# A decoder layer on one core: the static list of steps is made by playing their phases on the engines

## The chip, the cores and the metric

The kernel runs on one core of a Trainium2 chip. The metric is the device time of one execution in microseconds (us), the median over runs. The engines are named as in the profile: PE is TensorE, DVE is VectorE, ACT is ScalarE, POOL is GpSimd, SP is SyncE (here only a queue of DMA starts).

## What is computed

x is (4, 256, 256), a context is (4, 256, 128), all float32. Three blocks follow each other, each with a residual and a layer norm:

```python
x = layernorm(x + delta_rule_attention(x))          # 16 heads of 16, per batch, recurrent over 256 positions
x = layernorm(x + ssm(context, gate=x))             # selective scan, 16 states, 256 channels, y * silu(x)
x = layernorm(x + moe(x))                           # 2 shared + 16 routed experts, top 4, hidden 176
```

The SSM takes the attention's result only as its gate, so its recurrence depends on the context alone and can run beside attention. The experts need both.

## The kernel before, in words

**Attention** is a chain of steps per batch b = 0..3 (`ATTENTION`, L63 to L70): k, v, b, ssk, q, ssq project and normalise; P0 to P3 make products inside chunks of 16 positions; move_a sends them through DRAM (SP, L503 and L506) so that solve0 to solve2 (DVE, L1319 and L1320, 60 pairs of small instructions for four batches) can invert a triangular matrix per chunk; move_t sends the result back; tile_t spreads it for PE; UW0, UW1, H, GQ0, GQ1 are packed 32x32 products (L630); S1 to S14 are the recurrence over chunks, each a PE product and an ACT copy; O0, O1 give the output; ms normalises it (DVE L1386), wo projects it, ln and lnorm are the layer norm. Batches 0 and 2 are one chain, 1 and 3 another; each chain has one set of buffers.

**The SSM** is 32 iterations (2 halves of tokens by 16 states). `pre i` makes the inputs of iteration i+1: PE broadcasts B (L616), ACT copies it (L952) and takes the decays' exponentials (L961), POOL multiplies (L549), two buffers deep. `scan i` is the recurrence on DVE (L1273) and PE's broadcast of C (L623), which waits for the product of the iteration before; `add i` is DVE's product with C (L1281) and the sum (L1287). `y_out` closes a half. In front stand stack, dt0, dt1 and begin.

**The middle** of half 0: gate (SiLU of x on ACT, a product on DVE), yT, ynorm, x3T, gates0 to gates7 (top 4 of 16 by comparing all pairs; DVE L1429 to L1467), split (x into high and low parts, ACT L1084 and DVE L1416). gates0 may not start before `("y_out", 1)` (`NEEDS`, L87), because it writes into the SSM's buffers. The middle of half 1 goes beside the experts (`SIDE`).

**Experts**: PE's `hidden` and `outputs` (L809 to L834), ACT L1113, DVE L1477 and L1481, POOL L570. Before them the weights w1 are split: ACT copies to w1_hi (L1051), POOL subtracts to w1_lo (L556). w1_hi lies on the SSM's buffers, so this waits for the last y_out. In the kernel before the ACT part stands inside step `("tile_s", 3)`, L1046 to L1051.

**The order of the work.** Every engine's queue is written out in program order from one list, `STEPS = order()` (L122), and each engine takes from a step what is its own, so a DVE instruction that waits holds all later DVE instructions of the list. `order()` (L96) keeps one clock `now`. Each step has a PE time and a lateness; `now` goes on by the PE time and the chain may go on when `now` has passed its lateness:

```python
c = min(open_, key=lambda c: (max(ready[c], now), ["mid", "ssm", 0, 1].index(c)))
name, which, pe, late = chains[c].pop(0)
now = max(now, ready[c]) + pe
ready[c] = now + late
```

Ties go to the middle, then the SSM, then attention. SSM_PERIOD = 3.5 after each add, SECOND = 15 before chain 1 starts. `bank_turns()` (L127) follows the same list to give out PSUM banks.

Of the kernel before, what the change touches and what calls it, by code (L numbers as in the profile page):

```python
# [82 lines left out]

SSM_START = [("stack", 0, 3.5), ("dt0", 0.9, 8), ("dt1", 0.9, 12), ("begin", 0.5, 0.5)]
MIDDLE = [("gate", 0, 4), ("yT", 2, 3), ("ynorm", 0, 1), ("x3T", 2, 2)] + [(f"gates{i}", .2, 2) for i in range(GATE_PARTS)] + [("split", 0, 0)]

NEEDS = {"gate": {("lnorm", 0), ("lnorm", 1), ("y_out", 0)}, "gates0": {("y_out", NG - 1)}}  # L87

# [5 lines left out]


def order():  # L96

    chains = {x: [(n, b, pe, late) for b in range(x, B, 2) for n, pe, late in ATTENTION] for x in range(2)}  # L100
    chains[0] = chains[0][PRELUDE:]
    chains["ssm"] = [(n, 0, pe, late) for n, pe, late in SSM_START] + [s for i in range(NITER) for s in
                     [("pre", i, .5, 0), ("scan", i, .5, 0), ("add", i, 0, SSM_PERIOD)] + [("y_out", i // DS, 0, 4)] * (i % DS == DS - 1)]
    chains["mid"] = [(n, 0, pe, late) for n, pe, late in MIDDLE]
    ready = {0: 0, 1: SECOND, "ssm": 0, "mid": 0}
    done, steps, now = set(), [], 0
    while any(chains.values()):
        open_ = [c for c in chains if chains[c] and (c != "mid" or NEEDS.get(chains[c][0][0], set()) <= done)]
        c = min(open_, key=lambda c: (max(ready[c], now), ["mid", "ssm", 0, 1].index(c)))
        name, which, pe, late = chains[c].pop(0)  # L110
        now = max(now, ready[c]) + pe
        ready[c] = now + late
# [6 lines left out]

SECOND = 15  # L120
SSM_PERIOD = 3.5
STEPS = order()  # L122
MID_NAMES = [n for n, _, _ in MIDDLE]
SSM_NAMES = [n for n, _, _ in SSM_START] + ["pre", "scan", "add", "y_out"]


def bank_turns():  # L127
# [72 lines left out]
def decoder_layer(nc, x_tok_d, x_t_d, ctx_t_d, wqkvb_d, onorm_d, wo_d, inproj_d, convw_d, convb_d, xproj_d,  # L200
# [7 lines left out]
    with ExitStack() as ctx:  # L208
# [367 lines left out]
        def _(pe):  # L576
# [312 lines left out]
        def _(act):  # L889
# [23 lines left out]
            def prelude():  # L913
# [11 lines left out]
                for name, _, _ in ATTENTION[:PRELUDE]:  # L925
                    step(name, 0)
# [42 lines left out]
            def step(name, b):  # L969
# [74 lines left out]
                if name == "ln":  # L1044
                    rstd(x)
                if (name, b) == ("tile_s", B - 1):  # L1046

                    act.wait_ge(s_yout, 2 * NG)
                    act.wait_ge(s_ld_w1, LD_W1)
                    for kt in range(KT):  # L1050
                        act.activation(w1_hi[:, kt, :], w1[:, kt, :], ACT.Copy).then_inc(s_w1hi, 1)  # L1051

# [106 lines left out]
        def _(dve):  # L1159
# [47 lines left out]
            def prelude():  # L1207
# [24 lines left out]
                for name, _, _ in ATTENTION[:PRELUDE]:  # L1232
                    step(name, 0)
# [280 lines left out]
            for name, which in STEPS:  # L1514
# [10 lines left out]
                elif name == "y_out":  # L1525
                    y_out(which)
                elif name in MID_NAMES:
                    middle(name, which)
                elif name != "pre":
                    step(name, which)  # L1530
# [88 lines left out]
```

## Time and profile before

| what | us |
|---|---|
| median of 3 runs | 677.39 (673.43 to 677.89) |
| the profiled execution, its own time | 676.46 |
| its span in the trace | 674.7 |
| DVE busy | 427.9 (63%) |
| PE busy | 413.5 (61%) |
| ACT busy | 235.7 (35%) |
| POOL busy | 187.2 (28%) |
| chain that ended last: DVE, PE, issue, ACT | 50%, 25%, 10%, 8% |

Read it in stages. Up to 92 us inputs are loaded and the SSM is prepared beside the first attention steps; up to 345 us the 32 scans run with attention between them; up to 481 us attention of batches 2 and 3 runs with the middle; then the experts run to the end.

### The profile page before, as it was taken

The page shows a single profiled execution, that of the slowest core. Times are in us where ns is not written, and L with a number is a line of the kernel's source. Part 1 is how long each engine was busy: PE and PEld are TensorE (multiplying, and loading weights), DVE is VectorE, ACT ScalarE, POOL GpSimd, SP SyncE. Part 2 cuts the span into 40 slices and gives each one's busy share as a digit, 9 for nine tenths or more (in the row PEclk, how much of TensorE's full clock was granted, in tenths as well). Part 3 has the DMA queues.
Part 4 walks back from the last instruction along what each step waited for, and adds up shares of the span by engine and source line. Part 5 has one row for each costly group of instructions (what it writes and reads, how often), then busy time and mean ns, then how long its engine had stood idle before and what let it go on. Part 6 is the DMA issues. An engine that isn't in the chain of part 4 may idle for free.

```text
span 674.7 us, 18534 instructions
## 1 busy us (share of the span) xinstructions
PE 413.5 (61%) x8286; PEld 308.6 (46%) x8286; DVE 427.9 (63%) x608; ACT 235.7 (35%) x425; POOL 187.2 (28%) x100
## 2 busy tenths in 40 slices
PE   5656234612566646440578561654498999999994
PEld 3334122401343424220365450553376777778883
DVE  3554889999999987999865644210655566453334
ACT  3556245322334264531344521115243422122220
POOL 1000024421354433421200000005554563334441
PEclk9865757555555576655757555655689989999998
DMA  8001011001000000100100012502300000000000
GB/s 255 2 2 33 0 34 26 12 1 32 3 4 4 1 2 2 35 1 17 16 2 6 3 36 70 196 4 74 125 0 1 1 1 1 0 33 1 1 1 31
DMA packets 27962, 18.05 MB, mean 27 GB/s; under 512 B 19873, under 2 KB 25835, under 8 KB 27627
## 3 DMA queue, kind: packets, MB, share of 16 engines
q1 hardware_dynamic: 27723, 16.84, 8.4%
q8 instruction: 65, 1.06, 0.7%
q0 software_dynamic: 160, 0.04, 0.1%
q14 instruction: 14, 0.11, 0.1%
HBM read 13.66 MB, written 3.21 MB: 25 GB/s over the span
## 4 chain that ended last, share of the span: by engine, by line
DVE 50%; PE 25%; issue 10%; ACT 8%; POOL 2%; DMA 2%; SPq 1%; DVEq 1%; POOLq 0%; ACTq 0%
DVE arena_h L1273 12%; DVE arena_h L1287 8%; DVE arena_h L1281 6%; PE bank L630 4%; PE bank L834 3%; DVE tmp_o L1319 3%; DVE tt_s L1320 2%; PE bank L809 2%; PE bank L810 2%; PE bank L811 2%; POOL hg_lo L570 2%; PE bank L829 2%; PE bank L830 2%; DVE hg_hi L1481 2%; DVE ln_st L1191 1%
## 5 line engine op out<-in xcount | busy, mean ns | idle before, releaser
L549 POOL TENSOR_TENSOR arena_s<-du,bsb 128x1024 f32<-128x1024 f32 x32 | 86.3, 2696 | 240.9 <-ACT bsb L952 183.3
L570 POOL TENSOR_TENSOR hg_lo<-vkp,hg_hi 128x512 fp32r<-128x512 f32 x50 | 69.0, 1380 | 91.0 <-DVE hg_hi L1481 91.0
L1273 DVE TENSOR_TENSOR_SCAN arena_h<-arena_s 128x1024 f32<-128x1024 f32 x32 | 82.2, 2569 | 1.9 <-DVE ln_mv L1195 0.7
L1477 DVE TENSOR_TENSOR vkp<-vkp,bank 128x512 f32<-128x512 f32 x50 | 34.4, 687 | 72.0 <-ACT vkp L1113 71.3
L630 PE MATMUL bank<-vkp,tiles 32*32 32x32 f32 (+1 forms) x3072 | 52.6, 222 | 33.3 <-ACT tiles L966 20.6
L1113 ACT ACTIVATE vkp<-bank,b 128x512 f32<-128x512 f32 x50 | 34.3, 686 | 109.1 <-PE bank L811 108.8
L630 PEld LDWEIGHTS bank<-vkp,tiles 32*32 32x32 f32 x3072 | 47.3, 145 | 41.9 <-ACT tiles L966 22.8
L1287 DVE TENSOR_TENSOR arena_h<-arena_h 128x1024 f32<-128x1024 f32 x30 | 54.7, 1822 | 4.4
L623 PE MATMUL bank<-stk,eye 96*128 96x512 bf16 x32 | 18.8, 587 | 56.1 <-DVEq L1283 56.1
L961 ACT ACTIVATE arena_s<-delta,negA 128x510 f32<-128x510 f32 x64 | 42.3, 711 | 25.3 <-DVEq L1274 25.3
L556 POOL TENSOR_TENSOR w_lo<-w,w_hi 128x3200 fp32r<-128x3200 f32 x2 | 13.8, 6925 | 132.3 <-ACT w_hi L1051 132.3
L830 PE MATMUL bank<-w_lo,hg_hi 128*128 128x256 f32 x200 | 49.9, 283 | 0.0
L630 PE MATMUL bank<-qke,tiles 32*32 32x48 f32 (+1 forms) x1984 | 35.9, 233 | 20.6 <-issue 8.1
L630 PEld LDWEIGHTS bank<-qke,tiles 32*32 32x32 f32 x1984 | 32.7, 149 | 27.5 <-issue 17.7
L630 PE MATMUL bank<-tt_s,tiles 32*32 32x16 f32 x896 | 22.8, 212 | 35.5 <-ACT tt_s L1026 26.4
L1281 DVE TENSOR_TENSOR arena_h<-arena_h,bank 128x1024 f32<-128x1024 f32 x32 | 39.1, 1221 | 6.6 <-PE bank L623 2.1
L809 PE MATMUL bank<-x_hl,w_hi 128*128 128x512 f32 x100 | 41.9, 419 | 0.0
L810 PE MATMUL bank<-x_hl,w_hi 128*128 128x512 f32 x100 | 40.8, 408 | 0.0
L630 PEld LDWEIGHTS bank<-tt_s,tiles 32*32 32x32 f32 x896 | 17.2, 142 | 50.9 <-ACT tt_s L1026 32.7
L811 PE MATMUL bank<-x_hl,w_lo 128*128 128x512 f32 x100 | 40.4, 404 | 0.0
L830 PEld LDWEIGHTS bank<-w_lo,hg_hi 128*128 128x128 f32 x200 | 38.0, 190 | 1.0
L654 PE MATMUL bank<-xT,wqkvb 128*128 128x256 f32 x96 | 30.5, 479 | 9.1 <-DVEq L1175 9.1
(195 smaller groups left out, 851.8 us busy)
## 6 DMA issues: line engine op xcount, KB each, us to landing
w<-in_w SPq DMA_DIRECT2D x1, 3200.0 KB, 12.0
w<-in_w SPq DMA_DIRECT2D x3, 512.0 KB, 9.1
xT<-in_x_t SPq DMA_DIRECT2D x1, 1024.0 KB, 7.2
xres<-in_x_tok SPq DMA_DIRECT2D x1, 1024.0 KB, 8.8
scr_a<-at_g SPq DMA_DIRECT2D x4, 256.0 KB, 2.0
at_g<-scr_a SPq DMA_DIRECT2D x32, 32.0 KB, 2.1
scr_t<-tt_s SPq DMA_DIRECT2D x4, 256.0 KB, 2.0
at_g<-scr_t SPq DMA_DIRECT2D x32, 32.0 KB, 2.0
```

The lines of the kernel that those rows point to most:

```text
L549: pool.tensor_tensor(dBu[:, i % 2, :].rearrange("p (e t) -> p e t", e=2), du[:, :, GT_ * th:GT_ * th + GT_], bsb[:, i % 2, :].unsqueeze(1) ...
L570: pool.tensor_tensor(hg_lo[i % 2][:, :], hrel[:, i % 2, :], hg_hi[i % 2][:, :], ALU.subtract).then_inc(s_hglo, 1)
L630: mm = pe.matmul(o[r, at], tiles[x][k][r, half, c, :, :].rearrange("p g n -> p (g n)"), moving[r], start=start, stop=stop, skip_group_chec ...
L809: pe.matmul(o[:, :], w_hi, x_hl[th][:, 0, kt, :], start=(kt == 0), stop=False)
L810: pe.matmul(o[:, :], w_hi, x_hl[th][:, 1, kt, :], start=False, stop=False)
L811: mm = pe.matmul(o[:, :], w_lo, x_hl[th][:, 0, kt, :], start=False, stop=(kt == KT - 1))
L830: pe.matmul(o, h_hi, w_lo, start=False, stop=False, skip_group_check=True)
L961: act.activation(o, src, ACT.Exp, scale=negA[:, et, n:n + 1]).then_inc(s_dA, 1)
L1273: link(dve.tensor_tensor_scan(hst, dA[:, i % 2, :], dBu[:, i % 2, :], 0.0, ALU.mult, ALU.add))
L1281: link(dve.tensor_tensor(h_c, hst.rearrange("p (e t) -> p e t", e=2), bank_c[:, :].unsqueeze(1).broadcast_to([P, 2, GT_]), ALU.mult))
L1287: link(dve.tensor_tensor(ysum, ysum, hC, ALU.add))
L1477: link(dve.tensor_tensor(h, h, o[:, :], ALU.mult))
```

## The change

The two numbers beside each step are gone. A table `PHASES` gives for each step a sequence of stays on engines, and `order()` plays them: it keeps one clock for each of PE, ACT and DVE, and for each chain when its last step was issued and complete. It always takes the step that can start earliest; ties go to chain 0, chain 1, the SSM, the middle, w1. The split of w1 becomes a step of its own, after the last y_out. In every engine's code only the names follow; the instructions of a step are the same.

```diff
-SSM_START = [("stack", 0, 3.5), ("dt0", 0.9, 8), ("dt1", 0.9, 12), ("begin", 0.5, 0.5)]
+SSM_START = ["stack", "dt0", "dt1", "begin"]
+PHASES = {"k": "pe 2.6 act .8", "v": "pe 2.6 act 2.1 dve .9", "b": "pe 2.6 act 3.3", "ssk": "pe 1.5 dve .8 act 1.6 dve 1.7",
...
+          "tile_u": "act 1.5", "P": "pe 1.5 dve .7 act 1.1", "move_a": "dma 9.5", "move_t": "dma 9.5",
+          "solve0": "dve 4.9", "solve1": "dve 4.3", "solve2": "dve 6.8",
+          "UW": "pe 2 dve .8 act .5", "H": "pe 2.6 act .3", "GQ": "pe 2 dve 1.4", "S": "pe .5 act .3", "base": "pe 3", "O0": "pe 1.6",
...
+          "pre": "pe .6 act 2.1", "scan": "dve 2.5", "add": "dve 3.1", "y_out": "dve 1.6",
...
+EARLY = {"q", "P1", "P2", "P3", "UW1", "GQ0", "GQ1", "tile_u", "tile_s", "O1", "wo"} - {"wo"}
...
+NEEDS = {"gate": {("lnorm", 0), ("lnorm", 1), ("y_out", 0)}, "gates0": {("y_out", NG - 1)},
+         "w1": {("ln", B - 2), ("y_out", NG - 1)}}
...
+    chains["w"] = [("w1", 0)]
+    rank = [0, 1, "ssm", "mid", "w"]
+    engine = dict.fromkeys(["pe", "act", "dve", "dma"], 0.0)
...
+    def start(c):
+        name, which = chains[c][0]
+        at = issued[c] if name in EARLY else complete[c]
...
+        work = phases(name)
+        return max(at, engine[work[0][0]]) if work and work[0][0] != "dma" else at
+
     while any(chains.values()):
-        open_ = [c for c in chains if chains[c] and (c != "mid" or NEEDS.get(chains[c][0][0], set()) <= done)]
-        c = min(open_, key=lambda c: (max(ready[c], now), ["mid", "ssm", 0, 1].index(c)))
+        open_ = [c for c in rank if chains[c] and NEEDS.get(chains[c][0][0], set()) <= done]
+        c = min(open_, key=lambda c: (start(c), rank.index(c)))
...
+        for e, us in phases(name):
+            at = (max(at, engine[e]) if e != "dma" else at) + us
+            if e != "dma":
+                engine[e] = at
...
-                if (name, b) == ("tile_s", B - 1):
-
-                    act.wait_ge(s_yout, 2 * NG)
...
+            def split_w1():
+                act.wait_ge(s_yout, 2 * NG)
...
+                elif name == "w1":
+                    split_w1()
```

What the list becomes (both lists follow from the code by themselves):

| where in the list | before | after |
|---|---|---|
| scan 0 stands behind | solve2 of batch 0 | solve2 of batch 0 and P3 of batch 1 |
| last step of batch 0 (lnorm) stands behind | add 19 | add 5 |
| last step of batch 1 | add 30 | scan 11 |
| last step of batch 2 | the middle, no scan left | scan 17 |
| last step of batch 3 | the end of the list | add 25 |
| move_a, move_t of batch 3 | no scan left | add 15, scan 17 |
| scans with no attention between them | none | 27 to 31 |
| ynorm, x3T, gates0 to gates7, split | beside attention of batches 2 and 3 | the end of the list, alone |
| ACT's split of w1 | behind tile_s of batch 3 | right behind y_out 1 |

In the new list some attention steps stand next to each other on DVE with no scan between them: solve0 to solve2 of batch 0 around P of batch 1; solve0, solve1, UW, solve2, GQ (batches 1 and 0) with no scan before scan 1; solve0 to solve2 of batch 2 and of batch 3; UW, ssk, GQ of batches 2 and 3 before scan 13.

## Rows read from the trace of the kernel before

**Rows 1.** Windows: length, busy us of PE, PEld, DVE, ACT, POOL, then clock, DMA, GB/s.
```profile
0.00:92.40 92.40, 47.16 (x355) 27.09 (x355) 49.81 (x91) 43.35 (x66) 6.07 (x12) 0.76 0.19 57
92.40:345.00 252.60, 118.18 (x3757) 79.52 (x3757) 230.82 (x237) 100.23 (x200) 83.56 (x31) 0.57 0.05 11
345.00:486.00 141.00, 80.52 (x3186) 65.10 (x3186) 52.87 (x110) 42.70 (x89) 14.69 (x3) 0.56 0.19 62
481.40:674.70 193.30, 172.27 (x1004) 140.05 (x1002) 96.78 (x179) 51.42 (x75) 83.71 (x56) 0.96 0.02 6
```

**Rows 2.** Waits of DVE from 345 to 486 us: total, times, longest.
```profile
DVE tmp_o L1386 <- ACT v_w L1043: 34.9, 2, 24.8
DVE tiles L1374 <- PE bank L630: 14.3, 2, 11.6
DVE tmp_o L1319 <- DMA at_g<-scr_a: 9.1, 1, 9.1
```

**Rows 3.** The same of DVE from 92.4 to 345 us, its longest.
```profile
DVE arena_h L1281 <- PE bank L623: 2.1, 1, 2.1
```

**Rows 4.** Timeline of DVE: an iteration, ms of batch 0, a scan, ms of batch 3.
```profile
165.73 2.29 DVE L1273 TENSOR_TENSOR_SCAN arena_h<-arena_s 128x1024 f32<-128x1024 f32 x1
...
169.54 2.13 DVE L1287 TENSOR_TENSOR arena_h<-arena_h 128x1024 f32<-128x1024 f32 x1
171.70 2.29 DVE L1273 TENSOR_TENSOR_SCAN arena_h<-arena_s 128x1024 f32<-128x1024 f32 x1
...
221.20 0.75 DVE L1386 SCALAR_TENSOR_TENSOR tmp_o<-tmp_o,onorm,v_w 128x512 f32<-128x512 f32 x1
221.87 4.44 DVE L1273 TENSOR_TENSOR_SCAN arena_h<-arena_s 128x1024 f32<-128x1024 f32 x1
...
471.47 6.68 DVE L1386 SCALAR_TENSOR_TENSOR tmp_o<-tmp_o,onorm,v_w 128x512 f32<-128x512 f32 x1 [24.84 <-ACT v_w L1043]
```

**Rows 5.** Timeline of POOL: beside that scan, the w1 subtractions, the first of w2.
```profile
221.56 2.60 POOL L549 TENSOR_TENSOR arena_s<-du,bsb 128x1024 f32<-128x1024 f32 x1 [1.48 <-ACT bsb L952]
...
463.78 13.82 POOL L556 TENSOR_TENSOR w_lo<-w,w_hi 128x3200 fp32r<-128x3200 f32 x2 [132.31 <-ACT w_hi L1051]
485.12 4.16 POOL L563 TENSOR_TENSOR w_lo<-w,w_hi_b 128x512 fp32r<-128x512 f32 x2 [7.53 <-ACT w_hi_b L1102]
```

**Rows 6.** Timeline of PE: H of batches 0 and 3, scores, first hidden, first outputs.
```profile
120.29 3.38 PE L630 MATMUL bank<-k_uv,tiles 32*32 32x16 f32 x237 [2.40 <-ACT k_uv L1013]
125.29 0.50 PE L630 MATMUL bank<-k_uv,tiles 32*32 32x16 f32 x19 [1.62 <-issue]
...
349.33 3.59 PE L788 MATMUL bank<-cent,xT 128*128 128x16 f32 x16
...
429.84 0.73 PE L630 MATMUL bank<-k_uv,tiles 32*32 32x16 f32 x39 [1.36 <-ACT k_uv L1013]
...
436.20 1.37 PE L630 MATMUL bank<-k_uv,tiles 32*32 32x16 f32 x89 [1.55 <-issue]
...
481.43 0.99 PE L809 MATMUL bank<-x_hl,w_hi 128*128 128x512 f32 x1
...
489.71 0.36 PE L829 MATMUL bank<-w_hi_b,hg_hi 128*128 128x256 f32 x1 [3.49 <-DVE hg_hi L1481]
```

**Rows 7.** Timeline of ACT: table load before the sigmoid, split of w1.
```profile
353.01 1.28 ACT L1092 ACT_TABLE_LOAD   x1 [2.37 <-PE bank L788]
...
460.76 5.61 ACT L1051 ACTIVATE w_hi<-w 128x3200 fp32r<-128x3200 f32 x2
```

**Rows 8.** Timeline of DVE: a comparison of gates0, the first copy of gates6, split.
```profile
354.82 1.22 DVE L1430 TENSOR_TENSOR du<-sc 128x1024 f32<-128x1024 f32 x1
...
380.72 0.69 DVE L1458 CAST stk<-bank 96x512 bf16<-96x512 f32 x1 [1.70 <-ACT wb L1096]
...
387.62 1.22 DVE L1416 TENSOR_TENSOR x_hl<-xT,x_hl 128x1024 fp32r<-128x1024 f32 x1 [2.09 <-ACT x_hl L1084]
```

**Rows 9.** Costliest groups: the scans; busy, mean ns of one, idle before.
```profile
L1273 DVE TENSOR_TENSOR_SCAN arena_h<-arena_s 128x1024 f32<-128x1024 f32 x32 | 82.2, 2569 | 1.9 <-DVE ln_mv L1195 0.7
```

More of the change, by code:

```diff
@@ L82 @@
 GATE_PARTS = 8
-SSM_START = [("stack", 0, 3.5), ("dt0", 0.9, 8), ("dt1", 0.9, 12), ("begin", 0.5, 0.5)]
-MIDDLE = [("gate", 0, 4), ("yT", 2, 3), ("ynorm", 0, 1), ("x3T", 2, 2)] + [(f"gates{i}", .2, 2) for i in range(GATE_PARTS)] + [("split", 0, 0)]
-NEEDS = {"gate": {("lnorm", 0), ("lnorm", 1), ("y_out", 0)}, "gates0": {("y_out", NG - 1)}}
+SSM_START = ["stack", "dt0", "dt1", "begin"]
+MIDDLE = ["gate", "yT", "ynorm", "x3T"] + [f"gates{i}" for i in range(GATE_PARTS)] + ["split"]
+PHASES = {"k": "pe 2.6 act .8", "v": "pe 2.6 act 2.1 dve .9", "b": "pe 2.6 act 3.3", "ssk": "pe 1.5 dve .8 act 1.6 dve 1.7",
[6 rows of a table added]
+          "pre": "pe .6 act 2.1", "scan": "dve 2.5", "add": "dve 3.1", "y_out": "dve 1.6",
+          "gate": "act 3.9 dve 1.7", "yT": "pe 2 dve 3.8 act .6", "ynorm": "dve 2", "x3T": "pe 2 act 1.3",
+          "gates0": "pe 2 act 2.8 dve 1.5", "gates6": "pe .8 act .7 dve 2", "gates": "dve 1.4", "split": "act 1.1 dve 1.3"}
+EARLY = {"q", "P1", "P2", "P3", "UW1", "GQ0", "GQ1", "tile_u", "tile_s", "O1", "wo"} - {"wo"}
+INPUT_LAG = 1.9
+ROWS_OF_C = .6
+NEEDS = {"gate": {("lnorm", 0), ("lnorm", 1), ("y_out", 0)}, "gates0": {("y_out", NG - 1)},
+         "w1": {("ln", B - 2), ("y_out", NG - 1)}}
 SIDE = dict(zip([1, 3, 4, 6, 8, 10, 11, 12, 13, 14, 15, 17, 18],
@@ L93, with phases @@
 LAST_NORM_AT = 3
+def phases(name):
+    for key in (name, name.rstrip("0123456789")):
+        if key in PHASES:
+            words = PHASES[key].split()
+            return [(e, float(us)) for e, us in zip(words[::2], words[1::2])]
+    return []
 def order():
-    chains = {x: [(n, b, pe, late) for b in range(x, B, 2) for n, pe, late in ATTENTION] for x in range(2)}
+    chains = {x: [(n, b) for b in range(x, B, 2) for n in ATTENTION] for x in range(2)}
     chains[0] = chains[0][PRELUDE:]
-    chains["ssm"] = [(n, 0, pe, late) for n, pe, late in SSM_START] + [s for i in range(NITER) for s in
-                     [("pre", i, .5, 0), ("scan", i, .5, 0), ("add", i, 0, SSM_PERIOD)] + [("y_out", i // DS, 0, 4)] * (i % DS == DS - 1)]
@@ L104, in order @@
-    chains["mid"] = [(n, 0, pe, late) for n, pe, late in MIDDLE]
-    ready = {0: 0, 1: SECOND, "ssm": 0, "mid": 0}
-    done, steps, now = set(), [], 0
-    while any(chains.values()):
-        open_ = [c for c in chains if chains[c] and (c != "mid" or NEEDS.get(chains[c][0][0], set()) <= done)]
-        c = min(open_, key=lambda c: (max(ready[c], now), ["mid", "ssm", 0, 1].index(c)))
-        name, which, pe, late = chains[c].pop(0)
-        now = max(now, ready[c]) + pe
-        ready[c] = now + late
+    chains["ssm"] = [(n, 0) for n in SSM_START] + [s for i in range(NITER) for s in
+                     [("pre", i), ("scan", i), ("add", i)] + [("y_out", i // DS)] * (i % DS == DS - 1)]
@@ new lines, in order @@
+    chains["mid"] = [(n, 0) for n in MIDDLE]
+    chains["w"] = [("w1", 0)]
+    rank = [0, 1, "ssm", "mid", "w"]
+    engine = dict.fromkeys(["pe", "act", "dve", "dma"], 0.0)
+    issued, complete = dict.fromkeys(rank, 0.0), dict.fromkeys(rank, 0.0)
+    inputs, scanned = {0: 0.0}, 0.0
+    done, steps = set(), []
+    def start(c):
+        name, which = chains[c][0]
+        at = issued[c] if name in EARLY else complete[c]
+        if name == "pre":
+            at = max(issued[c], scanned)
+        if name == "scan":
+            at = inputs[which]
+        work = phases(name)
+        return max(at, engine[work[0][0]]) if work and work[0][0] != "dma" else at
@@ new lines, in order @@
+    while any(chains.values()):
+        open_ = [c for c in rank if chains[c] and NEEDS.get(chains[c][0][0], set()) <= done]
+        c = min(open_, key=lambda c: (start(c), rank.index(c)))
+        at = start(c)
+        name, which = chains[c].pop(0)
+        issued[c] = at
+        if name == "scan":
+            engine["pe"] = max(engine["pe"], complete[c]) + ROWS_OF_C
+        if name == "add":
+            at = max(at, engine["pe"])
+        for e, us in phases(name):
+            at = (max(at, engine[e]) if e != "dma" else at) + us
+            if e != "dma":
+                engine[e] = at
+        if name in ("begin", "pre"):
+            inputs[which + (name == "pre")] = at + INPUT_LAG
+        if name == "scan":
+            scanned = at
+        if name != "pre":
+            complete[c] = max(complete[c], at)
@@ L118 @@
 PRELUDE = 6
-SECOND = 15
-SSM_PERIOD = 3.5
 STEPS = order()
-MID_NAMES = [n for n, _, _ in MIDDLE]
-SSM_NAMES = [n for n, _, _ in SSM_START] + ["pre", "scan", "add", "y_out"]
+MID_NAMES = MIDDLE
+SSM_NAMES = SSM_START + ["pre", "scan", "add", "y_out", "w1"]
 def bank_turns():
@@ L1528, in _ @@
                     middle(name, which)
-                elif name != "pre":
+                elif name not in ("pre", "w1"):
                     step(name, which)
```

21 lines of the change are left out of this document (10 added, 11 removed), and 7 rows, old and new, of tables (ATTENTION, PHASES).

## The prediction

> **What bounds the kernel now.** I read the page first, then the windows by stage, then who waits for whom, then the timelines. The busy shares say little: DVE has 63% and PE 61%, and neither is full. The windows split it [rows 1]. From 92.4 to 345 us DVE is busy 230.8 of 252.6 us, 91%: all 32 scans run there, and DVE is the bound. From 345 to 486 us it is busy 52.9 of 141 us, 37%, and PE 57%: here no engine is full, and the latency of attention's chain for batch 3 is the bound. The waits of the second stage say so: DVE waited 34.9 us for ACT's result of ms, 14.3 us for GQ on PE and 9.1 us for the DMAs of move_a [rows 2], while the longest wait of the first stage was 2.1 us [rows 3]. From 481.4 us on the experts run, PE busy 172 of 193 us. So the order before spends its scans early, and when the last two batches wait for PE, ACT and DMA, nothing is left to fill DVE. That is where an order can gain: bring attention's latencies under the scans. It can't gain in the experts, and not below DVE's work.
>
> **The change, part by part.** No instruction is added or taken away. What changes is what stands behind what, on all queues. I work out when y_out 1 ends (call it T), then what stands between T and the experts, then the total.
>
> *Up to scan 0.* DVE reaches scan 0 at 92.4 us now, with 49.8 us of work [rows 1]. The new list puts P0 to P3 of batch 1 ahead of it; these are eight DVE instructions of some 0.29 us, 2.3 us. PE makes them while DVE solves batch 0, so I add only the 2.3: 94.7 us. Everything else of this stretch is the same work, and the ACT latencies of dt0 and dt1 stay open in it.
>
> *DVE's work from there to T.* Before, DVE did 230.8 + 52.9 = 283.7 us between 92.4 and 486 [rows 1]. From this come off: 2.3 for P of batch 1; 5.9, since ms of batch 3 took 6.68 us where ms of batch 0 takes 0.75 (it stood against POOL's w1 subtraction, which ran from 463.78 to 477.6) [rows 4, 5]; and 15.2 for what now stands behind T: ynorm 1.3, gates0 to gates4 6.4 (five of 1.22 and one of 0.23), gates5 2.0, gates6 1.7, gates7 1.8, split 1.2, and 0.8 of gaps counted with them (the pieces are the DVE rows from 354.56 to 388.84 that belong to gates and split, the dearest and the last stand in [rows 8]). Left: 260.3 us. In the dense stage DVE did its work at 91.4% [rows 1], the rest being the ends of instructions and short waits. At the same density 260.3 us take 285 us.
>
> *The waits that are new.* Batches 0 to 2 are now denser, so DVE meets waits that scans covered before. I follow the new list with these durations: H about 5.5 us from its release (120.29 to 125.8) [rows 6], GQ half of H, ms 9 to 10 us from the start of O0 (210.5 to 221.2 for batch 0) [rows 4], a move 7 to 10 us (DVE waited 9.1 for one) [rows 2], an iteration 5.97 us (165.73 to 171.70) [rows 4]. GQ of batch 0 stands right behind solve2 of batch 1 and comes 3.7 us late; GQ of batch 1 4.4; ms of batch 0 5.8 (only add 4 covers it), its wo 1.4; P of batch 2 2.0; ms of batch 1 1.0; GQ of batch 2 5.3 (only ssk of batch 3 covers H); P of batch 3 2.7; ms of batch 2, gate and yT together 5.0; UW of batch 3 and smaller ones 3.3; GQ of batch 3 3.5. That is 38 us. H took 7.8 us for batch 3 where PE showed pauses called issue (429.84 to 437.57) [rows 6], against 5.5 for batch 0; I add 5 us for such pauses in four batches. The extremes: at 0 the scans cover it all, and T is 380; at the density of the second stage now (37%) for all the attention work, there would be over 100 us of waits. I take 43, nearer to the first, since 26 of 32 adds still stand between attention steps, and no single wait before was longer than 2.1 us where scans stood between [rows 3].
>
> T = 94.7 + 285 + 43 = 422.7 us.
>
> *The tail of the list.* Between T and the experts nothing is left for overlap, while now gates run beside attention. ACT starts the split of w1 at T and POOL's subtractions start 3.0 us later and end at T + 16.8 (460.76, 463.78, 477.6) [rows 5, 7]. They don't bound: PE's first expert product needs also split, and that is a chain: ynorm 1.3; x3T behind ACT's 5.6 us of w1, to T + 7; scores 3.6 on PE [rows 6]; table load and sigmoid 1.5 [rows 7], so gates0 could start at T + 12.5. Its comparison has two operands in SBUF. The scan beside which POOL's product started 0.3 us earlier took 4.44 instead of 2.29 us [rows 4, 5], and ms took 6.68 instead of 0.75, until the subtraction was over. So I let gates0 wait for POOL: end of its first comparison T + 18.1, gates1 to gates4 T + 23.1, gates5 T + 25.3, gates6 with PE's transposes and ACT's copy 4.1 (T + 29.4), gates7 T + 31.3, split T + 33.6 (ACT's copy and DVE's 1.22, 2.3 from 386.53 on) [rows 8]. PE starts at T + 34 = 456.7 us, where it starts at 481.4 now [rows 6]: 24.7 us earlier. Without POOL's hindrance it would be T + 29.5, 4.5 us less.
>
> The Trainium skill, SBUF — State Buffer, Who interferes with whom, says that DVE and GpSimd share a port pair which one instruction holds for its whole length, the other being blocked fully. By that rule gates0 waits for the second subtraction to end, which is what I took from the two rows; by a rule of shared bandwidth the comparison would take about double, 1.2 us more, and the forecast would be 3 us lower. The trace agrees with the lock: 6.68 us ended 0.5 us after POOL did.
>
> *Behind it.* ACT's first split of w2 now starts before PE's first product, since nothing of attention stands in front, and the 4.16 us of POOL [rows 5] are out of the way sooner: outputs(0) comes 5 us behind the first product instead of 8.3 (481.4 to 489.7) [rows 6]: 3.3 us. The loads of w1 and w2 start earlier and were hidden. The experts are 193.3 us of the same instructions at clock 0.96.
>
> **Sum.** 676.46 - 24.7 - 3.3 = 648.5 us for an execution like the profiled one. That one is 0.93 us under the median, so 649.4; I say **649 us**, 4.2% less.
>
> **The rivals.**
>
> *A, the scans cover nearly everything.* The waits are under 20 us instead of 43, as in the dense stage now. For it: the longest wait there was 2.1 us [rows 3]. Against: there one or two attention steps stood between scans, now in places over ten. T = 380 to 395, the total 607 to 625.
>
> *B, slower: DVE stands in its own order.* DVE is in order. Wherever the table's time for PE is short of the chip's, a GQ or ms stands at the head of DVE with scans ready behind it, and no wait overlaps another. The table has 2.6 us for H, the trace 5.5 to 7.8 [rows 6]; UW, GQ, O and wo are short in the same way. In place of the 43 us put x: the kernel is slower when T passes 450.7, at x = 71, which is 18 us per batch. For it: the second stage shows 60 us of waits for two batches [rows 2], which nothing covered; all four batches at half of that give 120 x 0.6 = 72. Against: 26 iterations lie between. At x = 90 the total is 696. It decides with the tail: of the 105 us that batch 3 had alone, 34 come back behind T.
>
> *C, the scans get longer.* The 32 scans average 2.57 us where an undisturbed one takes 2.29 [rows 4, 9], 9 us in all; the one of 4.44 had POOL's product started just before it. The rule just cited speaks for more of these: the pre steps now stand behind attention's ACT work, so products start late. If every second scan pays 2.15 us, it is 34 us instead of 9: 25 more, total 674, no change to be told. Against: with nothing between, the iteration settles with POOL beside the adds, at 5.97 us [rows 4].
>
> *D, the change doesn't do what it says.* The chains don't run ahead on the chip as they do in the table, since the PE times in it are too short, and batch 3 ends late, with fewer scans beside it and S steps that wait for PE's broadcast of C. Half of the gain: 660 to 668.
>
> **How the numbers follow.** The forecast with its waits of 25 to 60 us (631 to 666): 0.55. A: 0.13. B: 0.13. C: 0.09. D: 0.10. A measurement of this kernel can tell about 1% from no change, 6.8 us. Faster by over 1% (under 670.6): all of the forecast, A, D and a third of C, 0.81. Within 1%: the rest of C and the near edge of B, 0.07. Slower by over 1%: 0.12. Leaving out the lower half of A and most of B gives 617 to 678.
>
> **What would show it.** In the new profile: scan 0 at about 95 us; the last scans 5.6 to 6.0 us apart with nothing of attention between them; L1386, L1374 and L1319 with several DVE waits of 1 to 6 us instead of few of 9 to 25; y_out 1 at 423 us, L1051 right behind it; one comparison of gates0 lengthened by POOL; PE's first L809 34 us later; experts of 190 us. I am wrong if DVE's share from scan 0 to y_out is over 87% (A) or under 74% (B), if the mean of L1273 goes over 3 us (C), or if y_out 1 comes before 450 us and the total is still not lower: then the tail or the experts have taken it.

## The result, and the profile after

The changed kernel is slower: 700.59 us, median of 4 runs (700.39 to 703.15), against 676.74 us for the kernel before, timed beside it. The ratio is 1.037, interval 1.0325 to 1.0414. The forecast was 649 us, its range 617 to 678. The profiled execution took 700.67 us with a span of 698.9, and what follows is compared with the 676.46 us and the span of 674.7 shown before.

The windows of the profile after, by stage (each row: length; busy time and number of instructions of PE, PE's weight loads, DVE, ACT, POOL; PE's granted clock; DMA share; GB/s). They are cut at scan 0, at the end of y_out 1 and at PE's first expert product:

```profile
0.00:102.20 102.20, 51.41 (x612) 31.25 (x612) 55.54 (x98) 51.78 (x84) 8.00 (x12) 0.75 0.19 54
102.20:476.60 374.40, 184.22 (x6644) 134.08 (x6644) 267.79 (x309) 125.36 (x262) 76.35 (x30) 0.56 0.10 30
476.60:510.50 33.90, 6.58 (x29) 5.74 (x29) 18.82 (x30) 12.51 (x11) 14.59 (x3) 0.50 0.00 0
510.50:698.90 188.40, 171.14 (x1002) 139.49 (x1002) 92.07 (x172) 49.67 (x72) 83.47 (x56) 0.96 0.02 6
```

In [rows 1] there was one stage with DVE at 91% and one with DVE at 37%. Now both are gone. Scans and attention lie over each other for 374 us, and DVE is busy 267.8 us of them, 71.5%. That is far from the 91% at which DVE was the bound: 106.6 us of DVE stand empty. The balance to the kernel before: scan 0 9.8 us later (102.2 for 92.4), from scan 0 to the experts 408.3 us for 389.0, so 19.3 more, and the experts 4.9 us shorter (188.4 for 193.3). 9.8 + 19.3 - 4.9 = 24.2, the difference of the spans.

The waits of DVE from 102.2 to 476.6 us, where before they were those of [rows 2] and [rows 3] (total, times, longest):

```profile
DVE tiles L1420 <- PE bank L675: 39.2, 8, 10.7
DVE tmp_o L1432 <- ACT v_w L1088: 18.9, 4, 7.6
DVE vkp L1404 <- PE bank L675: 5.7, 4, 2.0
DVE tiles L1414 <- PE bank L675: 5.0, 2, 2.6
```

L1420 is GQ's step on DVE (L1374 before), L1432 that of ms (L1386 before). The long wait of ms for batch 3, 24.8 us, and the 9.1 us for move_a are gone, as the change intends. In their place every batch waits for GQ, twice: 39.2 us in 8 waits, where the two batches of [rows 2] had 14.3. The timeline of DVE shows how these holes look: GQ of batch 1 and ms of batch 0, with the product with C and the sum of one iteration between them and no scan; then the longest wait, GQ of batch 2, and the scan behind it:

```profile
164.58 0.88 DVE L1420 SCALAR_TENSOR_TENSOR tiles<-bank,const 128x256 f32<-128x256 f32 x2 [8.09 <-PE bank L675]
...
169.09 0.88 DVE L1420 SCALAR_TENSOR_TENSOR tiles<-bank,const 128x256 f32<-128x256 f32 x2 [3.31 <-PE bank L675]
...
180.62 0.75 DVE L1432 SCALAR_TENSOR_TENSOR tmp_o<-tmp_o,onorm,v_w 128x512 f32<-128x512 f32 x1 [7.59 <-ACT v_w L1088]
181.29 2.28 DVE L1319 TENSOR_TENSOR_SCAN arena_h<-arena_s 128x1024 f32<-128x1024 f32 x1
...
289.72 0.88 DVE L1420 SCALAR_TENSOR_TENSOR tiles<-bank,const 128x256 f32<-128x256 f32 x2 [10.71 <-PE bank L675]
...
294.98 2.29 DVE L1319 TENSOR_TENSOR_SCAN arena_h<-arena_s 128x1024 f32<-128x1024 f32 x1 [0.22 <-DVE qke L1423]
```

The scans at 181.29 (scan 5) and 294.98 (scan 13) are the point. The first starts as ms ends, with no wait of its own. The last part of a scan's input is POOL's product, and POOL's timeline has those of scan 5 and scan 13:

```profile
154.53 4.09 POOL L594 TENSOR_TENSOR arena_s<-du,bsb 128x1024 f32<-128x1024 f32 x1 [10.18 <-ACT bsb L997]
...
262.95 2.35 POOL L594 TENSOR_TENSOR arena_s<-du,bsb 128x1024 f32<-128x1024 f32 x1 [19.93 <-DVEq L1320]
```

So the input of scan 5 was there from 158.6 us and that of scan 13 from 265.3. Both scans were ready for the whole of the 7.59 us and of the 10.71 us, and stood in DVE's queue behind the instruction that waited. On PE such a hole reads as follows (H, then both halves of GQ, here for batch 0):

```profile
117.38 1.78 PE L675 MATMUL bank<-k_uv,tiles 32*32 32x16 f32 x116 [1.40 <-ACT k_uv L1058]
119.66 1.91 PE L675 MATMUL bank<-k_uv,tiles 32*32 32x16 f32 x128 [0.50 <-issue]
123.39 0.34 PE L675 MATMUL bank<-k_uv,tiles 32*32 32x16 f32 x10 [1.82 <-issue]
...
127.49 1.94 PE L675 MATMUL bank<-vkp,tiles 32*32 32x32 f32 x128 [2.16 <-issue]
131.04 0.43 PE L675 MATMUL bank<-vkp,tiles 32*32 32x32 f32 x13 [1.61 <-issue]
```

From y_out 1 on the list went as forecast. y_out 1 and the gates' first step on DVE, then the split of w1 on ACT and POOL, then PE's first product of the hidden layer and of the outputs:

```profile
475.29 1.41 DVE L1341 SCALAR_TENSOR_TENSOR u<-u,dskip,arena_h 128x512 f32<-128x512 f32 x2
...
488.86 4.81 DVE L1475 TENSOR_TENSOR sc<-sig,ebias 128x64 f32<-128x64 f32 x1 [10.87 <-ACT sig L1136]
...
476.73 5.63 ACT L1095 ACTIVATE w_hi<-w 128x3200 fp32r<-128x3200 f32 x2 [13.83 <-DVE u L1341]
...
479.77 13.81 POOL L601 TENSOR_TENSOR w_lo<-w,w_hi 128x3200 fp32r<-128x3200 f32 x2 [15.73 <-ACT w_hi L1095]
...
510.49 0.77 PE L854 MATMUL bank<-x_hl,w_hi 128*128 128x512 f32 x1 [7.01 <-issue]
...
516.01 0.47 PE L874 MATMUL bank<-w_hi_b,hg_hi 128*128 128x256 f32 x1
```

From the end of y_out 1 (476.7) to PE's first expert product (510.5) it is 33.8 us. The last five scans stand 5.0 to 6.0 us apart, with nothing of attention between them.

### The profile page after: what moved, and what is told of

The parts are those of the page before. It is cut to its first block, busy times and chain, and to the rows that moved or that the text cites. A ratio compares the mean times of both kernels' runs of the same rounds, so it can differ in the third digit from the quotient of the medians.

```text
span 698.9 us, 18522 instructions
## 1 busy us (share of the span) xinstructions
PE 413.3 (59%) x8286; PEld 310.6 (44%) x8286; DVE 434.2 (62%) x608; ACT 239.3 (34%) x428; POOL 182.4 (26%) x100
## 4 chain that ended last, share of the span: by engine, by line
DVE 36%; PE 33%; ACT 13%; issue 13%; POOL 2%; DMA 1%; SPq 1%; DVEq 0%; POOLq 0%; ACTq 0%
PE bank L675 11%; DVE arena_h L1319 6%; DVE arena_h L1333 4%; DVE tmp_o L1365 4%; PE bank L879 3%; DVE arena_h L1327 3%; DVE tt_s L1366 3%; PE bank L699 2%; PE bank L854 2%; PE bank L855 2%; PE bank L856 2%; POOL hg_lo L615 2%; ACT arena_s L1006 2%; PE bank L874 2%; PE bank L875 2%
## 5 line engine op out<-in xcount | busy, mean ns | idle before, releaser
L594 POOL TENSOR_TENSOR arena_s<-du,bsb 128x1024 f32<-128x1024 f32 x32 | 81.0, 2532 | 378.7 <-ACT bsb L997 293.1
L1319 DVE TENSOR_TENSOR_SCAN arena_h<-arena_s 128x1024 f32<-128x1024 f32 x32 | 83.4, 2605 | 1.8 <-DVE qke L1423 0.4
L675 PE MATMUL bank<-vkp,tiles 32*32 32x32 f32 (+1 forms) x3072 | 54.0, 226 | 39.8 <-issue 20.6
L668 PEld LDWEIGHTS bank<-stk,eye 96*128 96x128 bf16 x32 | 3.5, 108 | 81.2 <-DVEq L1329 80.3
L699 PE MATMUL bank<-xT,wqkvb 128*128 128x256 f32 x96 | 32.7, 503 | 11.3 <-DVEq L1221 10.8
```

What stands on the lines that cost most here:

```text
L594: pool.tensor_tensor(dBu[:, i % 2, :].rearrange("p (e t) -> p e t", e=2), du[:, :, GT_ * th:GT_ * th + GT_], bsb[:, i % 2, :].unsqueeze(1) ...
L675: mm = pe.matmul(o[r, at], tiles[x][k][r, half, c, :, :].rearrange("p g n -> p (g n)"), moving[r], start=start, stop=stop, skip_group_chec ...
L699: mm = pe.matmul(to, w, xT[:, kt, cols], start=(kt == 0), stop=(kt == KT - 1))
L1319: link(dve.tensor_tensor_scan(hst, dA[:, i % 2, :], dBu[:, i % 2, :], 0.0, ALU.mult, ALU.add))
```

## The experiments

Ten kernels ran. None leaves work out; two issue a product twice, and in all others only the order of steps differs. Three theories stood at the start: the order puts no scan into the waits (it is static and DVE takes it in order), the table's times on TensorE are too short, or the priority of attention is wrong. The kernel before was timed anew with each group of runs, and every ratio is to that time.

**H twice, in each list.** H is the longest stay on TensorE ahead of a DVE step. Both kernels were given its products twice over:

```diff
-                    for half in range(2):
+                    for half in (0, 1, 0, 1):
                         for c in range(NC):
```

In the changed kernel:

> The changed kernel with the 256 matmuls of H issued twice in each batch (same result, the second pass writes the same again): 4 to 7 us more of PE four times, nothing else. Theory 1 (in the new list DVE stands still while PE works on H, in every batch): all of it is paid, 18 to 28 us more than the changed kernel, 718 to 729. Theory 2 (the loss lies elsewhere, H is covered by scans): under 10 us more.

In the kernel before:

> The same doubling of H in the kernel before. Theory 1 (there the scans cover PE in the dense stage and only batch 3, with no scans left, and partly batch 2 pay for it): 5 to 14 us more, 682 to 691. Theory 2 (both lists pay alike): 18 us or more.

Measured: 731.5 us (730.17 to 733.51) with the new list, 30.9 more than the 700.59 without (28.5 by the two ratios, 1.079 and 1.037), a little over the 18 to 28 expected; and 707.2 us (704.81 to 709.64) with the old one, 29.5 more than the 677.76 of the kernel before beside it. Both lists pay the same for what was added, so theory 2 of the second expectation holds. The waits of DVE in each, first of the new list from 102 to 508 us:

```profile
DVE tiles L1420 <- PE bank L675: 69.4, 8, 18.7
```

and of the old list from 92 to 345 us, then two of its longest behind that:

```profile
DVE arena_h L1281 <- PE bank L623: 14.2, 3, 6.2
...
DVE tiles L1374 <- PE bank L630: 21.2, 2, 18.5
DVE tmp_o L1340 <- PE bank L660: 14.1, 1, 14.1
```

In the new list the 30 us go straight to GQ (69.4 for 39.2). In the old one scans do stand behind H, but their product with C needs PE's broadcast, which is queued behind H on PE: L1281 waits 5.9 us in the first case. The scan behind H runs, and then its own next step waits for PE as GQ would: that scan covers 2.3 us of H, not the 6 of an iteration. This is the price of a longer H. H as it is was covered by the old list in its dense stage, where DVE waited at most 2.1 us [rows 3], and was not in the new one.

**TensorE's times in the table corrected.** Six entries (lines shortened):

```diff
-          "UW": "pe 2 dve .8 act .5", "H": "pe 2.6 act .3", "GQ": "pe 2 dve 1.4",
+          "UW": "pe 2.5 dve .8 act .5", "H": "pe 6.5 act .3", "GQ": "pe 3.8 dve 1.4",
...
-          "O0": "pe 1.6", "O1": "pe 1.6 act 1.3", "wo": "pe 2.4",
+          "O0": "pe 3.4", "O1": "pe 3.4 act 1.3", "wo": "pe 3.5",
```

> The changed kernel with six PE times in its table set to what the trace shows with the pauses called issue: H 6.5 for 2.6, GQ 3.8 for 2, UW 2.5 for 2, O0 and O1 3.4 for 1.6, wo 3.5 for 2.4. The instructions are the same, only the list's order follows. Theory 1 (the table's PE times are short, so DVE's queue has GQ and ms at its head while PE still works and scans stand behind): DVE's wait for PE at the GQ instructions falls from 39 us to under 20, the wait of ms from 19 to under 12, y_out 1 comes 15 to 30 us earlier, and the total is 672 to 687 us. Theory 2 (the waits come from putting attention ahead at all, whatever times the table has; a static list in which chains of such latency go first always parks DVE): the waits move but don't shrink, total 695 to 706.

Measured: 702.4 us (701.0 to 702.8), ratio to before 1.0355 (1.0334 to 1.0377), against 1.037 for the change as it is: nothing. The waits of DVE from 95 to 478.6 us:

```profile
DVE tiles L1420 <- PE bank L675: 32.2, 8, 8.8
DVE arena_h L1327 <- PE bank L668: 17.5, 2, 10.2
DVE tmp_o L1432 <- ACT v_w L1088: 14.7, 4, 7.5
```

11.2 us less in GQ and ms, and 17.5 us in two waits of the product with C that were 0.8 us in the change as it is. The holes moved, as theory 2 said. The new times also change which batches run side by side, and in this list scans 19 to 31 have no attention between them, where in the change it is scans 27 to 31. The table's sizes alone are not the cause; this run does not say that they are no part of it.

**The SSM ahead of attention.**

```diff
-    rank = [0, 1, "ssm", "mid", "w"]
+    rank = ["mid", "ssm", 0, 1, "w"]
```

> The changed kernel with one line changed: ties in the playing go to the middle and the SSM first, attention behind (the order of ranks of the kernel before). The scans then run one behind the other and nearly all of attention comes behind them. If the priority of attention was the fault, this is faster than the changed kernel, under 695; if scans are what fills attention's waits, it is far slower, 740 to 790 us: 32 scans of 6 us and then four batches in two chains of some 130 us each.

Measured: 798.2 us (two runs, 797.63 and 798.78), ratio 1.1795 (1.174 to 1.1849). The windows show why (the columns as above):

```profile
100.00:291.00 191.00, 31.70 (x70) 4.32 (x69) 179.95 (x102) 58.42 (x93) 70.68 (x30) 0.51 0.01 3
291.00:602.50 311.50, 149.65 (x6612) 125.62 (x6613) 102.87 (x248) 85.44 (x181) 13.83 (x2) 0.58 0.11 32
```

All scans run first at 94% of DVE, and attention's four batches then have DVE at 33%. It is slower still than the 740 to 790 expected. So attention ahead, taken as a whole, is not the fault; turning it about costs 98 us more than having it.

**The split of w1 alone, in the old list.** On ACT it goes from behind tile_s of batch 3 to behind tile_u of batch 3:

```diff
-                if (name, b) == ("tile_s", B - 1):
+                if (name, b) == ("tile_u", B - 1):
```

> The kernel before, with its own list, and only the split of w1 moved on ACT from behind tile_s of batch 3 to behind tile_u of batch 3, some 20 us earlier, where ACT has nothing to do. Theory 1 (POOL's subtraction of w1 held DVE's part of ms of batch 3 for 6 us): that instruction takes 0.75 us again in place of 6.68, and the total falls by 5 to 6 us, to 670 to 673. Theory 2 (the wait is covered by something else, or GQ of batch 3 is now held in its place): within 2 us of the kernel before.

Measured: 672.24 us (671.22 to 673.19), ratio 0.9919 (0.9894 to 0.9943), 5.5 us less, as theory 1 and the prediction's 5.9 for this item say. POOL's subtraction now stands under waits of attention (442.95 to 456.78), and ms of batch 3 takes what ms of batch 0 took in [rows 4], instead of 6.68:

```profile
472.98 0.75 DVE L1386 SCALAR_TENSOR_TENSOR tmp_o<-tmp_o,onorm,v_w 128x512 f32<-128x512 f32 x1 [25.66 <-ACT v_w L1043]
```

**Only the SSM's steps moved.** The order is given as a list. All steps of attention, of the middle and w1 keep their order from the change; the SSM's steps keep their order too and stand at other places between the rest, up to 21 steps earlier or 14 later, so that scans fall ahead of a DVE step that has to wait. stack and dt0 moved as well, which the expectation doesn't name. Around H of batch 2:

```diff
- ... scan.12 add.12 UW0.2 UW1.2 ssk.3 H.2 GQ0.2 GQ1.2 tile_u.2 q.3 S1.2 pre.13 scan.13 add.13 ...
+ ... pre.13 scan.13 add.13 UW0.2 UW1.2 ssk.3 pre.14 scan.14 add.14 pre.15 H.2 scan.15 GQ0.2 add.15 GQ1.2 tile_u.2 q.3 S1.2 ...
```

> The changed kernel with its list written out, and only the steps of the SSM's chain (dt1, begin, pre, scan, add, y_out) put elsewhere in it: 8 to 20 steps earlier or later, so that scan and add stand in front of the instructions on which DVE waits (scan 1 ahead of UW and H of batch 0, scan 15 behind H of batch 2, scans 18 to 25 spread over batch 3). Attention's, the middle's and w1's steps keep their order among themselves. Theory 1 (attention ahead is right, and the loss is that the played list puts no scan before the instruction that DVE waits for, since each scan ready then is put behind attention by a start a fraction of a microsecond later): the waits fall by half or more, y_out 1 comes before 445 us and the total is 640 to 665 us. Theory 2 (the list is bound by attention's latency, so that scans moved into waits lengthen the chain by as much): 690 to 705.

Measured: 646.22 us (645.26 to 646.71), ratio 0.9548 (0.9512 to 0.9583): 54 us less than the change with not one step of attention moved. Its window from scan 0 to y_out 1, two of DVE's waits there, and the timeline of DVE at GQ of batch 1 (8.09 us of wait above):

```profile
109.40:421.80 312.40, 172.58 (x6114) 123.61 (x6105) 253.19 (x272) 123.29 (x258) 74.29 (x30) 0.59 0.12 34
```

```profile
DVE tiles L1394 <- PE bank L649: 4.4, 3, 2.2
...
DVE tmp_o L1406 <- ACT v_w L1062: 3.3, 1, 3.3
```

```profile
146.84 3.17 DVE L1307 TENSOR_TENSOR arena_h<-arena_h 128x1024 f32<-128x1024 f32 x1
150.03 0.88 DVE L1394 SCALAR_TENSOR_TENSOR tiles<-bank,const 128x256 f32<-128x256 f32 x2
150.83 0.41 DVE L1397 TENSOR_TENSOR qke<-qke,bank 128x256 f32<-128x256 f32 x1
151.46 2.29 DVE L1293 TENSOR_TENSOR_SCAN arena_h<-arena_s 128x1024 f32<-128x1024 f32 x1 [0.22 <-DVE qke L1397]
153.90 1.22 DVE L1301 TENSOR_TENSOR arena_h<-arena_h,bank 128x1024 f32<-128x1024 f32 x1
```

GQ (L1394 here) waits 4.4 us in all instead of 39.2, ms 3.3 instead of 18.9, and DVE is busy 81% of the stretch. Sum, GQ, scan, product alternate: each short stay on DVE covers one on PE. The other waits changed little or grew: P and UW together wait 13.7 us for 10.7, the product with C 5.3 for 0.8. This is the theory shown directly: the chains' dependencies and PE's stays allow the overlap, and the list of the change does not use it. How such places are found is not shown; the list is given as it is.

**The gates moved too.** The SSM's steps, the middle ones and w1 stand elsewhere; attention keeps its order. ynorm and x3T go beside batch 3, and the end of batch 3 behind gates0 to gates4:

```diff
- ... scan.31 add.31 y_out.1 w1.0 ynorm.0 x3T.0 gates0.0 ... gates7.0 split.0
+ ... add.26 ynorm.0 ... pre.28 x3T.0 ... add.31 y_out.1 tile_s.3 gates0.0 ... gates4.0 w1.0 O0.3 gates5.0 O1.3 ms.3 gates6.0 gates7.0 split.0 wo.3 ln.3 lnorm.3
```

> As the run with moved scans, and the middle's steps and the split of w1 moved too, so that gates stand beside the last third of batch 3 (gates0 to gates4 ahead of O0, ms ahead of gates6). Attention's order is still that of the changed kernel. If the uncovered tail of 34 us is a part of the loss, this gives 15 to 27 us more than the run with moved scans, 620 to 645 us; if the gates now hold batch 3 by as much as they saved, within 5 us of it.

Measured: 629.7 us (628.3 to 631.59), ratio 0.9306 (0.9272 to 0.9341), 16.5 us under the run before it. y_out 1 ends at 408.6 for 421.8, and the tail to the first expert product is 28.9 us for 33.8.

**All free.** Every chain may move; each batch and the SSM keep their own sequence of steps. The list begins:

```
stack.0 dt0.0 tile_k.0 move_b.0 k.1 v.1 b.1 P0.0 P1.0 P2.0 P3.0 move_a.0 ssk.1 q.1 ssq.1 solve0.0 solve1.0 dt1.0 begin.0 solve2.0 pre.0
tile_k.1 scan.0 add.0 move_b.1 P0.1 move_t.0 tile_t.0 P1.1 P2.1 P3.1 pre.1 scan.1 add.1 UW0.0 UW1.0 pre.2 scan.2 add.2 pre.3 H.0
move_a.1 solve0.1 scan.3 add.3 pre.4 GQ0.0 GQ1.0 tile_u.0 S1.0 S2.0 S3.0 solve1.1 solve2.1 S4.0 ... S14.0 scan.4 tile_s.0 add.4 pre.5
O0.0 scan.5 move_t.1 add.5 pre.6 tile_t.1 O1.0 scan.6 add.6 pre.7 ms.0 UW0.1 scan.7 add.7 pre.8 UW1.1 wo.0 ln.0 scan.8 add.8 lnorm.0 ...
```

> A list in which all chains were free to move: batch 0 done at add 8, batch 1 at scan 16, the middle up to x3T before the last scans, gates between O and ms of batch 3, the last of attention behind the last scan. If density of DVE is what counts (no wait without a scan, no tail without work), DVE's share from scan 0 to the experts is over 83% and the total 595 to 625 us, under both kernels; if a chip with pauses on PE doesn't follow such a fine list, 640 or more.

Measured: 596.64 us (596.08 to 598.38), ratio 0.8821 (0.8791 to 0.885). It beats the kernel before by 11.8% and the change by 104 us. Its windows (from scan 0 to y_out 1, then to the first expert product) and, from 83.6 to 375.7 us, the longest waits of DVE:

```profile
83.60:375.70 292.10, 174.30 (x6660) 128.27 (x6663) 263.39 (x312) 129.56 (x273) 75.82 (x30) 0.60 0.11 29
375.70:404.60 28.90, 6.46 (x37) 3.74 (x30) 26.29 (x29) 9.56 (x8) 15.49 (x2) 0.56 0.34 115
```

```profile
DVE tiles L1388 <- PE bank L649: 3.5, 2, 2.8
DVE qke L1366 <- ACT tmp_o L1010: 2.9, 2, 1.4
```

DVE is at 90% up to y_out 1 and up to the experts, at the density of the dense stage of [rows 1] but with nearly all of attention under it. In the list H of batch 0 and GQ of batch 0 have solve0.1, scan 3 and add 3 between them, and O0 and ms of batch 0 have scans 5 and 6.

**Why the planner leaves the holes.** It takes the chain whose next step can start first, by the first phase of that step on whatever engine, and then books all of the step's phases. With a step that starts on PE its place in DVE's order is fixed too, and a scan that is ready a moment later on DVE comes behind it. Following `order()` of the change with its own table gives three ways into a hole:

- ms of batch 0 can start on PE at 119.9 and scan 5 on DVE at 120.1 (times of the table), so ms is taken, with its place on DVE. GQ of batch 1 (110.9) comes ahead of the product with C (112.2) in the same way.
- For GQ of batch 0, H ends at 81.4 by the table, while DVE is taken by solve2 until 85.1. The table sees no wait there. On the chip H takes 6.4 us where the table has 2.6, and this hole comes from the short time.
- Before GQ of batch 2, the longest wait, the SSM's next step is not scan 13 but pre 13, which starts on PE, and H and both halves of GQ tie with it (223.9, 226.5, 228.5). A tie goes to attention, and scan 13 waits behind pre 13 in its own chain.

One rule was added, which meets the first way: if the chosen step comes to DVE only later than the SSM's next scan, sum or y_out could start there, that one is taken first.

```diff
         c = min(open_, key=lambda c: (start(c), rank.index(c)))
+        if c in (0, 1, "mid") and chains["ssm"] and chains["ssm"][0][0] in ("scan", "add", "y_out"):
+            if start("ssm") < on_dve(c):
+                c = "ssm"
```

Here on_dve(c) adds up the phases of the step ahead of its first one on DVE.

> Edit: the changed kernel's own planner with one rule more: where the step that it chose comes to VectorE only after a later phase of its own (a product on TensorE first, as GQ, P and UW have), and the SSM's next scan, sum or y_out could start before that, the SSM's step is taken first. The times of the table stay. Theory (the planner compares steps by the start of their first phase, on whatever engine, and books the step's place in VectorE's order with it, so a scan that is ready a moment later is put behind a wait): that is why the static list leaves the waits open, and the rule closes many of them; the waits of GQ (39.2 us in 8) fall to 15 to 25 and the time to 660 to 685. Rival (the waits come from the table's short times on TensorE, from the priority of attention, or from the chains' dependencies, and how the planner compares steps is nothing): 695 to 705.

And the same rule with the corrected table:

> Edit: the rule of the run before and, in the table, TensorE's times as the trace has them (H 6.5, GQ 3.8, UW 2.5, O0 and O1 3.4, wo 3.5). Theory: with the rule in place the true times tell the planner how long a wait is, so they are worth something here, 5 to 15 us less than without them, though they were worth nothing alone (702.4). Rival: they are worth nothing here either, within 3 us of the run before.

Measured: 673.03 us (669.28 to 675.42, 10 runs), ratio 0.9954 (0.9921 to 0.9987), and 669.02 us (667.59 to 670.18), ratio 0.9888 (0.9833 to 0.9944). The rule takes back 27.6 us, which is all of the loss and a little more; the waits of DVE from 95 to 480 us begin with

```profile
DVE tiles L1432 <- PE bank L687: 29.7, 8, 7.6
DVE sc L1487 <- ACT sig L1148: 10.9, 1, 10.9
```

(the second is the gates' wait in the tail). GQ's 39.2 us fell to 29.7, a smaller fall than to the 15 to 25 expected, ms from 18.9 to 4.0. The first holes are still there: before scan 1, at 134.0 us, there is a gap of 31 us without a scan, where the free list runs scans 1 to 3 in the 31 us behind scan 0. By the table scan 1 has its input at 48.4 and could start on DVE at 85.1, just when GQ of batch 0 comes to it, and the rule asks for earlier. With the true times it stands ahead of GQ of batch 0. They are worth 4.0 us by the medians on top of the rule. The intervals of the two ratios overlap in part, so that step is near what these runs can tell; 5 to 15 was too much. The rule gets half the way to the 646 us of the list with moved scans. It is a less clean comparison than that one, since with it the steps of the two attention chains and of the middle also change their order among each other.

## Why the prediction was wrong

**Reading of the bound: right.** That the second stage was bound by latency and that it could be brought under the scans is what the free list shows: its experts start at 404.6 us for 481.4.

**Up to scan 0: 94.7 forecast, 102.2 measured, 7.5 us off.** I added only P of batch 1. The same list puts dt0 behind P of batch 0, v of batch 1 and move_a, and dt1 behind ssk and q of batch 1, where before dt0 stood behind the first P and dt1 behind the last, ahead of move_a. DVE's work on dt1 begins at 74.1 us instead of 64.4. POOL's products, which need it, then fall on the solve; the solve's first two products, and POOL beside them:

```profile
83.32 2.20 DVE L1365 TENSOR_TENSOR tmp_o<-at_g,tt_s 128x2 f32<-128x2 f32 x1
...
85.75 2.09 DVE L1365 TENSOR_TENSOR tmp_o<-at_g,tt_s 128x8 f32<-128x8 f32 x1
...
83.16 4.65 POOL L594 TENSOR_TENSOR arena_s<-du,bsb 128x1024 f32<-128x1024 f32 x2 [78.87 <-ACT bsb L997]
```

These two operations of 2 and 8 columns took 0.16 and 0.17 us before, so their lengthening alone is 4.0 us of the 7.5.

**DVE's work to y_out 1: 260.3 forecast, 267.8 measured, 7.5 more.** Of the items taken off, 0.8 us were gaps, which are not busy time; the others were about right, and ms of four batches takes 3.0 us for 8.9. The rest is longer operations. In this stretch the normalisation's L1250 takes 2.2 us more, the solve's products 1.6, the scans 1.2 and the copy that opens each half 1.1. Most of the L1250 is one pair that took 2.87 us for 0.73 while POOL's product of 262.95 ran; that the others too are POOL's doing is likely but not shown. (In the whole span, below, the solve's products take 31.7 us for 26.1, but 4.0 of that stand ahead of scan 0.) Groups of DVE after (busy, mean ns, idle before), the scan's to be set beside [rows 9]:

```profile
L1319 DVE TENSOR_TENSOR_SCAN arena_h<-arena_s 128x1024 f32<-128x1024 f32 x32 | 83.4, 2605 | 1.8 <-DVE qke L1423 0.4 <-DVE ln_mv L1241 0.2 <-DVE qke L1392 0.2
...
L1365 DVE TENSOR_TENSOR tmp_o<-at_g,tt_s 128x2 f32<-128x2 f32 (+14 forms) x60 | 31.7, 528 | 2.0
...
L1250 DVE TENSOR_SCALAR xres<-xres,ln_mv,ln_r 128x256 f32<-128x256 f32 x24 | 12.6, 578 | 1.0 <-ACT ln_r L1104 0.7 <-DVE ln_mv L1241 0.2
```

**The waits that are new: the step that failed.** I put 38 us, and 5 for PE's pauses, on top of the 24.7 that a density of 91.4% leaves idle: 67.7 us of idle DVE. Measured are 106.6, 39 more. So the term that I set at 43 is 82, over the 71 us from which rival B says slower. (It is what is left when the 24.7 are taken off; the waits of DVE for other engines in this stretch, added up as they stand, are 89 us.) GQ was to cost 16.9 (3.7, 4.4, 5.3, 3.5) and cost 39.2; ms was to cost at most 11.8 (5.8, 1.0 and a part of 5.0) and cost 18.9. These two make 29 of the 39 us. Two things were wrong in GQ's figure, and each is half of the error. I gave GQ of a batch one wait, worked out from the tail of H; it has two, since its halves are two stays on PE with DVE's step behind each, 3.6 to 4.5 us apart: the second waits are 11.1 us. And the first waits are 28.1 us (4.98, 8.09, 10.71, 4.35) for 16.9. I gave H 5.5 us and half of it to GQ, where H took 6.4 us for batch 0 (117.38 to 123.73) and both GQ 7.9 (123.60 to 131.47). For the pauses I added 5 us; PE's rows of waits, from 102.2 to 476.6 us, say

```profile
PE bank L675 <- issue: 41.2, 29, 2.2
```

against 29.0 us in 24 pauses from 92.4 to 486 before, 12.2 us more; how much of that DVE paid is not shown. I had the right row [rows 6] and took the shorter of its two cases. The last 10 us of the 39 are not split further; the longest wait to which I gave no term is that of the first DVE step of ssq of batch 2, 4.6 us.

The forecast is then 7.5 + 7.5 + 39 = 54 us off at y_out 1: 476.7 for 422.7. The tail and the experts give back 1.8, which makes the 52.2 us between 648.5 and 700.7.

**The tail: right.** 33.8 us for 34, and the first outputs 5.5 us behind the first product for 5. POOL held DVE there as I took it to: the operation of 128x64 that met it took 4.81 us, where it took 0.23 before, and ended at 493.67, POOL at 493.58. It was the addition ahead of the comparison, not the comparison. The experts take 188.4 us, where 193.3 less 3.3, 190.0, was forecast.

**The rivals.** B is what happened: 71.5% of DVE, under its line of 74%. That 700.7 us lie near its 696 at x = 90 is partly chance: x was 82, which gives 688 by its sum, and the rest are the two errors of 7.5 us. Its mechanism is right: DVE stands in its own order with scans ready. Its reason, the table's short times for PE, is a part of it: it makes the hole at GQ of batch 0, but the corrected table alone gave 702.4 and no gain, and with the rule it gave 4.0 us. D's half gain (660 to 668) was not met either. C fell: the scan's mean is 2605 ns for 2569. A did not come with this list, but its 607 to 625 us are not out of reach of the program: 596.6 were measured with another order of the same instructions.

The argument against B, that 26 iterations lie between attention's steps, counted scans and not their places, and it is what kept the term at 43. The kernel with only scans moved has the same 32 iterations, ends y_out 1 at 421.8 us (the 422.7 of the forecast, by a sum that this list doesn't earn) and takes 646.2. I had worked out about what a list of this kind could reach and not what this list does. The place was seen (GQ of batch 2, 5.3 us, "only ssk of batch 3 covers H"), but its price was not worked out stay by stay: H and both halves of GQ are three stays on PE with nothing of DVE between them, and cost 10.7 and 2.6 us there.

**What stays open.** Beside the 4.0 us in two lengthened operations, where the rest of scan 0's 7.5 us comes from was not tried apart. No run changes only who wins a tie at a place such as GQ of batch 2, so what each of the three ways into a hole costs is not known. Nor was it tried why PE pauses in H and GQ.

## What to carry to other kernels

A planner for engines that run in order must compare its candidates at the place that they take in the queue of the bound engine, not by when their first phase may start on another; a rule of a dozen lines for that was worth 27.6 us here. The change's own order of attention with its scans at other places gave 27 us more than that (646.2), and moving gates and attention too another 50 (596.6). Before trusting that a denser order covers a latency, look in the list, for each step that waits, at which long operation stands directly ahead of it on that engine and whether that operation's own next input is queued on the engine that is waited for. Make the true time of every stay part of it, but expect little from correcting the table while the rule of choice is blind to the wait. And look at what a tie does: a step that only prepares the next scan can hold back the scan that is ready.

## What the runs showed of the hardware that was not expected

PE pauses in long rows of small products. A row of 113 to 128 products of 32x32 by 16 or 32 columns takes 1.7 to 1.9 us and is followed, in three of the four cases shown (the fourth: 0.5 us), by 1.6 to 2.2 us in which PE waits for nothing that the profile shows; H and both GQ of batch 0 took 14.1 us, of which 6.1 are four pauses. Issuing H twice cost some 30 us in four batches, 7.5 each, in a list with scans close by as in one without; in the first the time stood in the scans' own waits for PE's broadcast (14.2 us up to 345 us) and in attention's.

POOL's products lengthen even DVE's smallest operations: 128x2 from 0.16 to 2.20 us. The Trainium skill, SBUF — State Buffer, Who interferes with whom, gives the rule for it: an operation of DVE with two operands in SBUF and one of GpSimd that reads SBUF exclude each other for the whole length of the one that came first. The trace agrees with it: the 2.20 us ended as the first of POOL's two products did (half of 4.65 us behind 83.16), and the 4.81 us ahead of the gates 0.09 us after POOL's.
